# A two-layer graph network: pattern of the scatters, PSUM places of a step and the place of its additions

## The chip, the cores and the metric

The kernel runs on one core of a Trainium2 chip. The metric is the device time of one execution in microseconds, as the median of several executions.

## The reference

A graph of 6250 nodes with 128 channels and 206250 directed edges, sorted by their target `dst`, goes through two layers. The first takes the mean of the neighbours' rows, two products and a log-softmax. The second, in which the change lies, computes for each edge a weight row from 64 edge attributes (two products with a ReLU between), multiplies it with the row `h[col]` of the edge's target, and adds the result up by the edge's source.

```python
def reference(x, src, dst, edge_attr_64, ...):
    def _L1_gnn_ref(x, edge_index, edge_rbf, W1, b1, W2, b2, Wl, bl):
        weight = jnp.maximum(edge_rbf @ W1 + b1, 0.0) @ W2 + b2
        h = x @ Wl + bl
        row, col = (edge_index[0], edge_index[1])
        msg = h[col] * weight
        out = jax.ops.segment_sum(msg, row, num_segments=x.shape[0])
        return out
    edge_index = jnp.stack([src, dst])
    h = jnp.maximum(_layernorm(x, axis=-1), 0.0)
    x = x + _L0_gnn_ref(h, edge_index, L0_gnn_W_l, L0_gnn_W_r, L0_gnn_b)
    h = jnp.maximum(_layernorm(x, axis=-1), 0.0)
    x = x + _L1_gnn_ref(h, edge_index, edge_attr_64, L1_gnn_W1, ...)
    return x
```

## The kernel before

The work has three stages. The first two (layer 0, and the normalised rows `h` of layer 1 as three bf16 parts, `h1p`) are not touched. The third computes the messages of layer 1 and sums them by source.

**Steps.** The edges stand in 1664 tiles of 128 (NS = SB * P slots with the filling). Four tiles make a step, so G = 416 steps, of which 403 (GT) cover the edges' own tiles; all engines walk the same list of steps, written by `steps` (line 299): four single steps, then six parts (LOOPS, line 44), each of which but the first opens with 12 steps written out, followed by a loop of rounds of 16 steps, and 16 steps written out at the end. The order on each engine is written by hand in its own `layer1`, and semaphores (in `S`) tie the engines together. Index s or g is the step; `wait` leaves out waits on zero or less.

**A step on PE** (line 1282): `node_rows(s)` picks the rows `h[col]` with one-hot matrices into pHG; `ranks(s + 1)` counts, for the next step, how many edges of each source block come ahead of each edge, into pQ; `weights(s)` makes the weight rows of the step into pW (four times 128 channels, one PSUM bank; two places, used in turn); `hidden(s + 1)` and `attr_T(s + 2)` prepare the weights of later steps; then, in steps that carry an octet, `sums`.

**A step on ACT** (line 1457): `rows_copy` (line 1439, pHG to SBUF), `local_rows`, `stream_hot` (half of the one-hot rows of an octet, lines 1451 and 1455), `relu(s + 1)`, `attrT_copy(s + 2)`.

**A step on DVE** (line 1021): `block_hot(s + 2)`, `one_hot_T(s + 1)`, `stream_hot` (the other half of the octet's one-hot rows), `block_adds` of the octet before, `messages(s)` (line 989: pW times the copied rows, into the ring `outr` of U = 4 steps), and `row_places(s + 1)`, which ends with the slot numbers `idxr` of step s + 1 (line 983). That last instruction waits until the scatters that last used the same place of the ring, four steps back, have landed (line 982).

**POOL** (line 590) waits for the slot numbers, the source numbers (`local_rows`) and the messages of a step and scatters its four tiles into the stream `messages` in HBM, sorted by blocks of 128 sources: four indirect DMAs of 128 rows of 129 floats. The stream is zeroed beforehand; a scatter writes its rows or adds them, and `adding` says which of the four add. Four first steps and a first loop of 4 rounds of 12 steps use `fewer`, in turn one and two adding ones of four; a second loop of GL - 4 rounds of 12 steps (GL, line 33, is (GT - 1 - U) // (3 * U)) and the last 16 steps use the default, two of four.

**Octets.** When a part of the edges has been scattered, its part of the stream is read back while the next part is computed: an octet is eight tiles of it, loaded by SP (line 427) and summed by source on PE with one-hot matrices (`sums`, line 1272) into pFL, one PSUM bank with four sums of pairs of tiles; DVE adds each to its block of X (`block_adds`, line 1010, four additions, line 1016, whose block numbers are loaded into registers first). In a loop, three steps of four carry an octet. In these steps `sums` waits until the additions of the octet before have read pFL (line 1294). The last part's octets follow behind the steps, in pF.

PSUM has eight banks: 0 pTP, 1 and 2 pHID, 3 and 4 pW, 5 pHG, 6 pQ, 7 pFL.

The lines that the change and the prediction's steps touch are 261 and 264 (places), 606 to 619 (POOL's loops), 985 to 990 (`messages`), 1021 to 1034 (DVE's order), 1238 to 1247 (`weights`) and 1282 to 1295 (PE's order).

Of the kernel before, what the change touches and what calls it, by code (L numbers as in the profile page):

```python
# [5 lines left out]
def gnn_program(nc, x, src, dst, edge_attr, W_l, W_r, b_0, W1, b1, W2, b2, Wl, bl, out):  # L6
# [7 lines left out]
    P = 128  # L14
    N, C = x.shape
# [9 lines left out]
    J = 4  # L25
    GE = J * P
    U = 4
# [15 lines left out]
    FO = 8  # L43
# [43 lines left out]
    with ctx:  # L87
# [88 lines left out]
        onesb = sb("onesb", [P, P], bf16)  # L176
# [4 lines left out]
        W2s = sb("W2s", [P, C], fp32)  # L181
# [35 lines left out]
        hidT = part(big, used, 2 * GE).rearrange("p (s e) -> p s e", s=2)  # L217
        hgs = part(big, used, 2 * GE).rearrange("p (s f) -> p s f", s=2)
        outr = part(big, used, U * J * ROW).rearrange("p (u j c) -> p u j c", u=U, j=J)
# [23 lines left out]
        PS = pb("PS", [P, 8, 512], fp32)  # L243
# [14 lines left out]

        pTP = PS[:, 0, 0:2 * P].rearrange("p (q e) -> p q e", q=2)
        pHID = PS[:, 1:3, 0:2 * P]  # L260
        pW = PS[:, 3:5, :]
        pHG = PS[:, 5, :]
        pQ = PS[:, 6, 0:5 * NBK].rearrange("p (j b) -> p j b", j=5)
        pFL = PS[:, 7, :]
        pF = PS[:, 0:4, :]

        names = """raw_in w_in consts srcs_ready big_zero keys_ready keys_out offs_out off_in off_ready
# [18 lines left out]
        def wait(eng, s, v):  # L286

            if not (isinstance(v, int) and v <= 0):
                eng.wait_ge(s, v)
# [186 lines left out]
        def _(pool):  # L476
# [113 lines left out]
            def scatter(g, n, adding=(1, 3)):  # L590
                if not isinstance(g, int):
                    pool.wait_ge(S["rank_chain"], placed)
                    pool.reg_add(placed, placed, 5)
                    pool.wait_ge(S["lrow_ready"], lrows)
                    pool.reg_add(lrows, lrows, 1)
                    pool.wait_ge(S["msg_done"], filled)
                    pool.reg_add(filled, filled, 1)
                else:
                    pool.wait_ge(S["rank_chain"], 5 * g + 5)
                    pool.wait_ge(S["lrow_ready"], g + 1)  # L600
                    pool.wait_ge(S["msg_done"], g + 1)
                for j in range(J):
                    pool.indirect_dma_start(strm_d, bass.IndirectOffsetOnAxis(ap=idxr[:, n % U, j:j + 1], axis=0),  # L603
                                            outr[:, n % U, j, :], None, compute_op=ALU.add if j in adding else ALU.bypass).then_inc(S_sc[n % U], 16)
# [9 lines left out]
                    scatter(None, U + k, fewer[k % 2])  # L614
            with pool.Fori(0, GL - RINGS * LOOPS[0] // 3):
                for k in range(3 * U):
                    scatter(None, U + k)
            for g in range(U + GL * 3 * U, G):
                scatter(g, g)

# [9 lines left out]
        def _(dve):  # L630
# [339 lines left out]
            def row_places(g, n):  # L970
                k, s = n % U, n % 2
                dve.wait_ge(S["rank_done"], g + 1)
                wait(dve, S["rank_chain"], g * 5)
                nc.vector.tensor_tensor(place[:, 0, :, :], pQ[:, 0:J, :], taken.unsqueeze(1).to_broadcast([P, J, NBK]), ALU.add)\
                    .then_inc(S["rank_chain"], 1)
                dve.wait_ge(S["rank_chain"], g * 5 + 1)
                nc.vector.tensor_tensor(place[:, 1, :, :], place[:, 0, :, :], hotW[:, s, 1:, :], ALU.mult).then_inc(S["rank_chain"], 1)
                dve.wait_ge(S["rank_chain"], g * 5 + 2)
                nc.vector.tensor_reduce(place_f, place[:, 1, :, :], AX, ALU.add).then_inc(S["rank_chain"], 1)
                nc.vector.tensor_tensor(taken, taken, pQ[:, J, :], ALU.add).then_inc(S["rank_chain"], 1)  # L980
                dve.wait_ge(S["rank_chain"], g * 5 + 3)
                wait(dve, S_sc[k], (g - k) * 16)
                nc.vector.tensor_copy(idxr[:, k, :], place_f).then_inc(S["rank_chain"], 1)  # L983

            def messages(g, n):
                k = n % U
                dve.wait_ge(S["w_done"], g + 1)
                dve.wait_ge(S["hgc_done"], g + 1)
                nc.vector.tensor_tensor(outr[:, k, :, 0:C], pW[:, k % 2, :].rearrange("p (j c) -> p j c", j=J),  # L989
                                        hgs[:, k % 2, :].rearrange("p (j c) -> p j c", j=J), ALU.mult).then_inc(S["msg_done"], 1)  # L990

            one_hot_T(0, 0)
# [17 lines left out]
            def block_adds(i, sums):  # L1010
                dve.load(pair_regs, bq_i[0:1, ds(i * (FO // 2), FO // 2)])
                ats = [dve.snap(pair_regs[r], min_val=0, max_val=(NB - 1) * C) for r in range(FO // 2)]
                dve.wait_ge(S["finmm_done"], i + 1)
                for r, at in enumerate(ats):
                    wait(dve, S["fadd_done"], i * (FO // 2) + r)
                    nc.vector.tensor_tensor(Xf[:, ds(at, C)], Xf[:, ds(at, C)], sums[:, r * C:(r + 1) * C], ALU.add)\  # L1016
                        .then_inc(S["fadd_done"], 1)

            adding = [None]

            def layer1(s, n, o):
                more = not isinstance(s, int) or s + 1 < G
                if not isinstance(s, int) or s + 2 < G:
                    block_hot(s + 2, n + 2)
                if more:
                    one_hot_T(s + 1, n + 1)
                if o:
                    stream_hot(*o)
                if adding[0]:
                    block_adds(adding[0][0], pFL)  # L1030
                adding[0] = o
                messages(s, n)
                if more:
                    row_places(s + 1, n + 1)

            def next_part(p):
                dve.wait_ge(S["rank_chain"], 5 * TURN[p - 1])
# [15 lines left out]
        def _(pe):  # L1053
# [184 lines left out]
            def weights(g, n):  # L1238
                k = n % U
                pe.wait_ge(S["relu_done"], g + 1)  # L1240
                wait(pe, S["msg_done"], g - 1)
                nc.tensor.matmul(pW[:, k % 2, :].rearrange("p (j c) -> p j c", j=J), onesb[0:3, :],  # L1242
                                 bp[:, 2, :].unsqueeze(1).to_broadcast([3, J, C]), start=True, stop=False)
                for j in range(J):
                    last = nc.tensor.matmul(pW[:, k % 2, j * C:(j + 1) * C], hidT[:, k % 2, j * P:(j + 1) * P], W2s[:, :],  # L1245
                                            start=False, stop=(j == J - 1))
                last.then_inc(S["w_done"], 1)

# [33 lines left out]
            def layer1(s, n, o):  # L1282
                k = n % U
                known = isinstance(s, int)
                node_rows(s, k)
                if not known or s + 1 < G:
                    ranks(s + 1, n + 1)
                weights(s, k)
                if not known or s + 1 < G:
                    hidden(s + 1, (k + 1) % U)  # L1290
                if not known or s + 2 < G:
                    attr_T(s + 2, (k + 2) % U)
                if o:
                    wait(pe, S["fadd_done"], o[0] * (FO // 2))
                    sums(*o, pFL)

            steps(pe, layer1)

# [199 lines left out]
```

## Time and profile before

| | us |
|---|---|
| median of 3 executions | 3839.27 |
| lowest, highest | 3835.75, 3843.43 |
| the profiled execution | 3873.64 |
| its span, first to last instruction | 3871.5 |
| busy: PE, DVE, POOL, ACT | 3140.0, 2756.7, 2322.5, 2022.3 |
| POOL's scatters (line 603), 1664 | 2151.4 |

The profile is of one execution on the chip. A row of a timeline gives the start in us from the first instruction, the duration in us, the engine, the line, the operation, what it writes and reads, how many were merged, and in brackets how long the engine had been idle and what ended that. A wait is put down to the engine whose signal came last; "issue" is time in which the engine waited for nothing that the profile shows, and "remote" a signal whose sender isn't known. PE's ends are modelled. Register loads, waits and the issuing of DMAs are not counted as busy time; on POOL the scatter's own instruction is.

### The profile page before, as it was taken

Reading aid. Unit: us, or ns where it says so; the run is one execution under the profiler, and the core shown is the slowest. Engines: PE = TensorE matmul, PEld = TensorE weight load, DVE = VectorE, ACT = ScalarE, POOL = GpSimd, SP = SyncE. Lnnn points to the kernel's source line nnn. Section 1 sums busy time; section 2 is a strip of 40 time slices with the busy share of each in tenths; the row PEclk is TensorE's granted clock in tenths of the full one; section 3 lists DMA queues with packets and bytes.
Section 4 is the critical chain, followed back from the end, with each engine's and each line's share of the span. In section 5 each row is a group of like instructions: output and inputs, shape, how many; then the busy total and the mean of one; then the engine's idle time right before and its main releaser. Section 6 shows DMA issues by size and latency. Waiting matters only on the chain.

```text
span 3871.5 us, 95963 instructions
## 1 busy us (share of the span) xinstructions
PE 3140.0 (81%) x26010; PEld 2539.7 (66%) x26011; DVE 2756.7 (71%) x7612; ACT 2022.3 (52%) x4679; POOL 2322.5 (60%) x1790
## 2 busy tenths in 40 slices
PE   1799999997677888887888877888788887888867
PEld 1699999996455566665666656666566665666656
DVE  8899999997654466665666666666566665666646
ACT  2699899984422244544444444444344443444456
POOL 4310100102377778888887788888888888888830
PEclk9999999997777688998898989899898998999989
DMA  3399999201144466666676666666666666666757
GB/s 105 96 331 322 319 320 321 90 3 34 38 83 81 82 144 135 147 128 136 139 149 133 137 129 147 145 139 141 127 144 142 141 142 122 144 142 141 151 131 207
DMA packets 578296, 572.22 MB, mean 148 GB/s; under 512 B 69883, under 2 KB 562035, under 8 KB 577986
## 3 DMA queue, kind: packets, MB, share of 16 engines
q1 hardware_dynamic: 431314, 449.42, 40.9%
q0 software_dynamic: 146672, 119.07, 20.4%
q8 instruction: 147, 2.41, 0.3%
q14 instruction: 163, 1.33, 0.1%
HBM read 283.37 MB, written 284.85 MB: 147 GB/s over the span
## 4 chain that ended last, share of the span: by engine, by line
PE 46%; issue 18%; DVE 13%; POOL 7%; ACT 5%; another core or an unknown queue 5%; DMA 4%; DVEq 2%; ACTq 0%; SPq 0%; POOLq 0%
PE PS L1278 10%; PE PS L1115 10%; PE PS L1245 7%; POOL messages L603 6%; PE PS L1257 5%; PE PS L1106 4%; PE PS L1234 3%; DMA messages<-big,idxr 3%; DVE aux L767 2%; ACT big L1451 2%; DVE X L1016 2%; PE PS L1242 2%; PE PS L1226 2%; ACT hpar L1455 1%
## 5 line engine op out<-in xcount | busy, mean ns | idle before, releaser
L603 POOL DMA_INDIRECT messages<-big,idxr x1664 | 2151.4, 1293 | 570.5 <-issue 467.7
L1278 PE MATMUL PS<-big,hpar 128*128 128x128 f32 x4800 | 661.5, 295 | 227.8 <-ACT hpar L1455 120.9
L1278 PEld LDWEIGHTS PS<-big,hpar 128*128 128x128 f32 x4800 | 618.6, 208 | 278.4 <-issue 248.3
L1439 ACT ACTIVATE big<-PS 128x512 f32<-128x512 f32 x416 | 248.5, 597 | 986.3 <-PE PS L1257 635.1
L989 DVE TENSOR_TENSOR big<-PS,big 128x512 f32<-128x512 f32 x416 | 287.4, 691 | 474.9 <-PE PS L1245 222.2
L1115 PE MATMUL PS<-h_parts,counts 128*128 128x258 f32 x3626 | 565.0, 296 | 0.0
L1245 PE MATMUL PS<-W2s,big 128*128 128x128 f32 x3328 | 557.9, 318 | 0.0
L1355 ACT ACTIVATE counts<-PS 128x784 fp32r<-128x784 f32 x592 | 481.8, 825 | 119.1 <-PE PS L1106 115.0
L1245 PEld LDWEIGHTS PS<-W2s,big 128*128 128x128 f32 x3328 | 468.8, 218 | 108.5 <-issue 108.5
L1428 ACT ACTIVATE big<-PS,b1c 128x512 f32<-128x512 f32 x416 | 283.7, 682 | 455.7 <-PE PS L1234 247.7
L1016 DVE TENSOR_TENSOR X<-X,PS 128x128 f32 x1200 | 345.2, 288 | 247.8 <-PE PS L1278 84.3
L1115 PEld LDWEIGHTS PS<-h_parts,counts 128*128 128x128 f32 x3626 | 469.9, 191 | 0.2 <-ACT counts L1355 0.2
L1257 PE MATMUL PS<-hpar,big 128*128 x4992 | 418.0, 230 | 56.2 <-issue 53.8
L507 POOL DMA_INDIRECT KLg<-edge_keys,tj_i x37 | 69.8, 1886 | 625.4 <-PE PS L1086 597.8
L1257 PEld LDWEIGHTS PS<-hpar,big 128*128 128x128 bf16 x4992 | 362.6, 103 | 94.0 <-issue 65.4
L767 DVE TENSOR_TENSOR aux<-iotaLq,cols 128x1024 bf16<-128x1024 bf16 x592 | 407.9, 689 | 0.4
L1451 ACT ACTIVATE big<-iotaF,big 128x128 f32<-128x128 f32 x1200 | 380.7, 390 | 42.9 <-DMA big<-messages 41.2
L1106 PE MATMUL PS<-aux 128*128 128x98 bf16 x4736 | 316.4, 211 | 62.0 <-DVE aux L767 58.1
L1234 PE MATMUL PS<-big,W1s 64*128 64x256 f32 x1664 | 343.1, 494 | 0.0
L767 DVE TENSOR_TENSOR aux<-iotaKq,cols 128x784 bf16<-128x784 bf16 x592 | 342.2, 578 | 0.0
L1264 PE MATMUL PS<-big,onesb 128*128 128x250 bf16 x416 | 122.0, 293 | 242.3 <-DVE idxr L983 116.8
L1106 PEld LDWEIGHTS PS<-aux 128*128 128x128 bf16 x4736 | 243.1, 99 | 99.4 <-DVE aux L767 77.1
(222 smaller groups left out, 3768.4 us busy)
## 6 DMA issues: line engine op xcount, KB each, us to landing
messages<-zeros SPq DMA_DIRECT2D x843, 193.5 KB
big<-messages SPq DMA_DIRECT2D x300, 516.0 KB
aux<-slot_rows SPq DMA_DIRECT2D x416, 128.0 KB
big<-in_edge_attr_dram SPq DMA_DIRECT2D x402, 128.0 KB
messages<-big,idxr POOLq DMA_INDIRECT x1664
X<-in_x_dram SPq DMA_DIRECT2D x12, 448.0 KB, 7.2
out_dram<-X SPq DMA_DIRECT2D x6, 448.0 KB
edge_places<-big SPq DMA_DIRECT2D x1, 2496.0 KB, 13.3
```

What stands on the lines that cost most here:

```text
L603: pool.indirect_dma_start(strm_d, bass.IndirectOffsetOnAxis(ap=idxr[:, n % U, j:j + 1], axis=0), outr[:, n % U, j, :], None, compute_op=AL ...
L767: last = nc.vector.tensor_tensor(oh[:, o % NOH, :, :, :], numbers.unsqueeze(1).to_broadcast([P, Q // few, width, few]), cols[:, n % 2, w, ...
L989: nc.vector.tensor_tensor(outr[:, k, :, 0:C], pW[:, k % 2, :].rearrange("p (j c) -> p j c", j=J), hgs[:, k % 2, :].rearrange("p (j c) -> p ...
L1016: nc.vector.tensor_tensor(Xf[:, ds(at, C)], Xf[:, ds(at, C)], sums[:, r * C:(r + 1) * C], ALU.add)\
L1106: last = nc.tensor.matmul(psB[:, o % 2, s, 0:KD], ohl[:, o % NOH, s // IL, :, s % IL], ohk[:, o % NOH, s // IK, :, s % IK], start=True, st ...
L1115: last = nc.tensor.matmul(psD[:, h, :], Bc[h][:, b, :], h0p[:, b, :], start=(b == 0), stop=(b == NB - 1))
L1234: last = nc.tensor.matmul(pHID[:, h, :].rearrange("p (q e) -> p q e", q=2), W1s[h * R:(h + 1) * R, :], attrT[h * R:(h + 1) * R, k % 2, :, ...
L1245: last = nc.tensor.matmul(pW[:, k % 2, j * C:(j + 1) * C], hidT[:, k % 2, j * P:(j + 1) * P], W2s[:, :], start=False, stop=(j == J - 1))
L1257: last = nc.tensor.matmul(pHG[:, j * C:(j + 1) * C], oht[:, k % 2, j * P:(j + 1) * P], h1p[:, ds(at + a * C, C)], start=(a == 0), stop=(a ...
L1278: last = nc.tensor.matmul(to[:, r * C:(r + 1) * C], finhot[:, n % 2, r * 2 + q, :], fin[:, k, r, q * ROW:q * ROW + C], start=(q == 0), sto ...
L1355: nc.scalar.activation(Bc[h][:, :, o * Q * D:(o + 1) * Q * D].rearrange("p b (s d) -> p b s d", s=Q), psB[:, o % 2, :, 0:KD].rearrange("p ...
L1451: last = nc.scalar.activation(away[:, t, :], iotaF[:, :], ACT.Abs, bias=fin[:, k, r, q * ROW + C:(q + 1) * ROW])
```

## The change

POOL's second loop gets the pattern of its first: in turn one and two adding scatters of four. pW shrinks to one bank, so that `weights` of step g waits until `messages` of step g - 1 have read it, instead of step g - 2. The bank that comes free becomes a second place of pFL, used in turn by the octets, so that `sums` waits for the additions of the octet before last. In DVE's order `block_adds` moves from ahead of `messages` to the end of the step, behind `row_places`.

```diff
--- before.py
+++ after.py
@@ -258,10 +258,10 @@
 
         pTP = PS[:, 0, 0:2 * P].rearrange("p (q e) -> p q e", q=2)
         pHID = PS[:, 1:3, 0:2 * P]
-        pW = PS[:, 3:5, :]
+        pW = PS[:, 3, :]
         pHG = PS[:, 5, :]
         pQ = PS[:, 6, 0:5 * NBK].rearrange("p (j b) -> p j b", j=5)
-        pFL = PS[:, 7, :]
+        pFL = [PS[:, 4, :], PS[:, 7, :]]
         pF = PS[:, 0:4, :]
 
         names = """raw_in w_in consts srcs_ready big_zero keys_ready keys_out offs_out off_in off_ready
@@ -614,7 +614,7 @@
                     scatter(None, U + k, fewer[k % 2])
             with pool.Fori(0, GL - RINGS * LOOPS[0] // 3):
                 for k in range(3 * U):
-                    scatter(None, U + k)
+                    scatter(None, U + k, fewer[k % 2])
             for g in range(U + GL * 3 * U, G):
                 scatter(g, g)
 
@@ -986,7 +986,7 @@
                 k = n % U
                 dve.wait_ge(S["w_done"], g + 1)
                 dve.wait_ge(S["hgc_done"], g + 1)
-                nc.vector.tensor_tensor(outr[:, k, :, 0:C], pW[:, k % 2, :].rearrange("p (j c) -> p j c", j=J),
+                nc.vector.tensor_tensor(outr[:, k, :, 0:C], pW.rearrange("p (j c) -> p j c", j=J),
                                         hgs[:, k % 2, :].rearrange("p (j c) -> p j c", j=J), ALU.mult).then_inc(S["msg_done"], 1)
 
             one_hot_T(0, 0)
@@ -1026,12 +1026,12 @@
                     one_hot_T(s + 1, n + 1)
                 if o:
                     stream_hot(*o)
-                if adding[0]:
-                    block_adds(adding[0][0], pFL)
-                adding[0] = o
                 messages(s, n)
                 if more:
                     row_places(s + 1, n + 1)
+                if adding[0]:
+                    block_adds(adding[0][0], pFL[adding[0][1] % 2])
+                adding[0] = o
 
             def next_part(p):
                 dve.wait_ge(S["rank_chain"], 5 * TURN[p - 1])
@@ -1238,11 +1238,11 @@
             def weights(g, n):
                 k = n % U
                 pe.wait_ge(S["relu_done"], g + 1)
-                wait(pe, S["msg_done"], g - 1)
-                nc.tensor.matmul(pW[:, k % 2, :].rearrange("p (j c) -> p j c", j=J), onesb[0:3, :],
+                wait(pe, S["msg_done"], g)
+                nc.tensor.matmul(pW.rearrange("p (j c) -> p j c", j=J), onesb[0:3, :],
                                  bp[:, 2, :].unsqueeze(1).to_broadcast([3, J, C]), start=True, stop=False)
                 for j in range(J):
-                    last = nc.tensor.matmul(pW[:, k % 2, j * C:(j + 1) * C], hidT[:, k % 2, j * P:(j + 1) * P], W2s[:, :],
+                    last = nc.tensor.matmul(pW[:, j * C:(j + 1) * C], hidT[:, k % 2, j * P:(j + 1) * P], W2s[:, :],
                                             start=False, stop=(j == J - 1))
                 last.then_inc(S["w_done"], 1)
 
@@ -1291,8 +1291,8 @@
                 if not known or s + 2 < G:
                     attr_T(s + 2, (k + 2) % U)
                 if o:
-                    wait(pe, S["fadd_done"], o[0] * (FO // 2))
-                    sums(*o, pFL)
+                    wait(pe, S["fadd_done"], (o[0] - 1) * (FO // 2))
+                    sums(*o, pFL[o[1] % 2])
 
             steps(pe, layer1)
 
```

## Rows read from the trace of the kernel before

**Rows 1.** The page: span, busy time by engine, slices of POOL.

```profile
span 3871.5 us, 95963 instructions
...
PE 3140.0 (81%) x26010; PEld 2539.7 (66%) x26011; DVE 2756.7 (71%) x7612; ACT 2022.3 (52%) x4679; POOL 2322.5 (60%) x1790
...
POOL 4310100102377778888887788888888888888830
```

**Rows 2.** Windows: stretch, us; busy us (count) of PE, PEld, DVE, ACT, POOL; clock, DMA, GB/s.

```profile
1066.00:1372.00 306.00, 245.66 (x1392) 165.59 (x1392) 150.22 (x481) 79.81 (x191) 232.56 (x192) 0.72 0.44 83
1400.00:2030.00 630.00, 516.88 (x3905) 396.46 (x3903) 417.73 (x1315) 286.88 (x725) 510.56 (x393) 0.90 0.68 140
2030.00:2200.00 170.00, 143.88 (x1017) 110.82 (x1018) 109.25 (x342) 76.74 (x195) 130.82 (x103) 0.85 0.64 135
2200.00:3540.00 1340.00, 1095.07 (x8321) 838.31 (x8321) 891.48 (x2793) 605.44 (x1537) 1087.04 (x831) 0.91 0.67 139
```

**Rows 3.** POOL's timeline: start, us, instruction, idle time before; first loop of scatters.

```profile
1107.24 0.98 POOL L603 DMA_INDIRECT messages<-big,idxr  x1 [0.31 <-issue]
...
1109.79 1.60 POOL L603 DMA_INDIRECT messages<-big,idxr  x1 [0.30 <-issue]
...
1114.24 1.66 POOL L603 DMA_INDIRECT messages<-big,idxr  x1 [0.30 <-issue]
...
1117.49 1.57 POOL L603 DMA_INDIRECT messages<-big,idxr  x1 [0.30 <-issue]
1119.36 0.98 POOL L603 DMA_INDIRECT messages<-big,idxr  x1 [0.30 <-ACT big L1433]
```

**Rows 4.** POOL's timeline in the second loop of scatters.

```profile
2040.25 0.98 POOL L603 DMA_INDIRECT messages<-big,idxr  x1 [0.30 <-issue]
2041.54 1.56 POOL L603 DMA_INDIRECT messages<-big,idxr  x1 [0.30 <-issue]
...
2052.86 0.97 POOL L603 DMA_INDIRECT messages<-big,idxr  x1 [0.30 <-issue]
```

**Rows 5.** Timeline, all engines: scatters that ran beside an issue of SP.

```profile
1879.15 0.38 SPq L427 DMA_DIRECT2D big<-messages  x1
1879.26 1.23 POOL L603 DMA_INDIRECT messages<-big,idxr  x1 [0.30 <-issue]
...
2003.02 2.01 POOL L603 DMA_INDIRECT messages<-big,idxr  x1 [0.30 <-issue]
```

**Rows 6.** Waits from 1380 to 3600 us: who <- whom, us, times, longest.

```profile
POOL messages L603 <- issue: 388.3, 1273, 0.7
...
DVE idxr L983 <- DMA messages<-big,idxr: 144.7, 100, 5.5
...
DVE X L1016 <- PE PS L1278: 71.9, 86, 2.4
...
POOL messages L603 <- DVE big L989: 23.3, 51, 1.6
...
PE PS L1278 <- DVE X L1016: 15.4, 19, 1.4
```

**Rows 7.** Timeline of all engines over one step with an octet.

```profile
1882.19 0.69 DVE L989 TENSOR_TENSOR big<-PS,big 128x512 f32<-128x512 f32 x1 [0.74 <-PE PS L1245]
...
1882.56 2.02 PE L1278 MATMUL PS<-big,hpar 128*128 128x128 f32 x16 [0.81 <-ACT hpar L1455]
...
1883.98 0.17 DVE L983 CAST idxr<-big 128x4 int32<-128x4 f32 x1
...
1885.25 0.28 PE L1264 MATMUL PS<-big,onesb 128*128 128x250 bf16 x1
...
1885.96 1.55 DVE L1016 TENSOR_TENSOR X<-X,PS 128x128 f32 x4
...
1888.37 1.80 PE L1278 MATMUL PS<-big,hpar 128*128 128x128 f32 x14 [0.35 <-ACT hpar L1455]
1888.70 0.69 DVE L989 TENSOR_TENSOR big<-PS,big 128x512 f32<-128x512 f32 x1 [1.19 <-remote]
```

## The prediction

> **What bounds the kernel now.** I read the page first, for the share of each engine and for the slices, then the windows of the third stage (the 416 steps of four tiles each), then POOL's timeline, then the waits, and last one step of all engines. On the page POOL is busy for only 60% of the span and PE for 81% [rows 1], which would name PE. The slices say otherwise: POOL's digits are 7 to 9 from the twelfth slice to the next to last, and POOL counts as idle in the 0.30 us before each scatter, which no other engine ends [rows 3, 4]. Adding that: a step has four scatters, and between 1400 and 2030 us POOL issued 393 of them in 630 us, busy 510.56 us [rows 2]; 393 x 0.30 us = 118 us of issue makes 628.5 of 630 us. POOL does nothing else than scatter, back to back. 393/4 = 98.25 steps in 630 us are 6.41 us a step; from 2200 to 3540 us it is 1340/207.75 = 6.45. I use 6.43.
>
> The waits agree. POOL waited for the products (line 989) 23.3 us in 2220 us, and its own issue makes 388.3 us; in the other direction, DVE's write of the next slot numbers (line 983) stood 144.7 us, 100 times, until a scatter had landed [rows 6]. The rest of the step runs ahead of POOL and is held back by the ring of four. Spread over the (3600 - 1380)/6.43 = 345 steps of that window this is 0.42 us a step: an estimate of what the other engines have in hand. The exception is 2030 to 2200 us: 103 scatters in 170 us, 6.60 us a step, with TensorE's granted clock at 0.85 of full speed [rows 2]; there the others had fallen back and POOL waited.
>
> **The scatters.** The change gives the steps of POOL's second loop the pattern that its first loop has. GL is (403 - 1 - 4) // 12 = 33, the first loop takes 4 rounds, so 29 rounds x 12 = 348 steps move from two accumulating scatters of four to three of eight; the last 16 steps stay. Number and bytes of the scatters stay too. Both patterns stand in the trace without a disturbance. With three of eight, eight scatters take from 1107.24 to 1119.36 us, 12.12 us [rows 3]; with four of eight, from 2040.25 to 2052.86 us, 12.61 us [rows 4]. That is 6.06 against 6.305 us a step, 0.245 us less. It is less than the plain difference of one scatter: an accumulating one takes 1.56 us and a plain one 0.98 [rows 4], 0.58 us per two steps, but behind two plain ones the accumulating one took 1.60 and 1.66 us, and the one behind a single plain one 1.57 [rows 3]. So 348 x 0.245 = 85 us, and without that after-effect 174 x 0.58 = 101 us; I take 85, since the after-effect is in the rows of the same pattern.
>
> The measured 6.43 is 0.125 us above the undisturbed 6.305. Part of it are scatters that ran long while SP issued another DMA: a plain one of 1.23 us started 0.11 us after the issue of a stream load [rows 5]. The number of stream loads a step doesn't change, so I keep the whole 0.125 us; the first loop has no stream loads and can't show whether it grows. New floor of POOL: 6.06 + 0.125 = 6.185 us a step.
>
> **Whether the others follow.** 0.245 us a step is less than the 0.42 us they have in hand, so POOL stays the bound on average. But what is in hand isn't spread evenly: the stretch at 2030 to 2200 us had none, and 170/6.6 = 26 steps there gain nothing, 26 x 0.245 = 6 us. With a faster POOL such stretches start earlier and last longer. I count them twice over, 13 us, and a floor between none and the whole gain is what the range has to carry.
>
> **One PSUM place for the weights** (lines 1241 to 1246, 989). `weights` of step s now waits until the products of step s - 1 have been read. Ahead of it on PE's queue stand `node_rows` and `ranks` of s + 1, and `ranks` already waits for the slot numbers of step s, which DVE makes after the products of step s - 1, in order. In the step shown, DVE's line 983 starts at 1883.98 us, `ranks` (line 1264) runs at 1885.25, and the products ahead of line 983 had started at 1882.19 [rows 7]: the new wait is met before PE comes to it. Cost 0; were the order of PE's queue another, it would be the 0.69 us of the products a step, on PE.
>
> The Trainium skill speaks against this edit: Perfetto Trace Analysis, section Matmuls, says that independent matmul groups should rotate through different PSUM banks, so that reading one overlaps the matmuls of the next. By that rule the 0.69 us would stand on PE in each step, which is worked out in rival (a); the trace doesn't agree, as the reading is over before the next group starts, so the sum holds 0 for it.
>
> **Two places for the sums, additions last in the group** (lines 264, 1029 to 1034, 1294). `sums` now waits for the additions of the octet before last. The wait that this loosens is small: PE stood 15.4 us for line 1016 in the whole window; what `sums` waits for is mostly ACT's one-hot rows. DVE stood 71.9 us for `sums` ahead of the additions [rows 6], and the products stood behind them on DVE's queue. Moved behind `row_places`, the additions (four of 0.29 us and their gaps, 1.55 us [rows 7]) find their sums long done, and the products and slot numbers, which POOL wants, come up to 1.55 us earlier in a step with additions. Queued behind the additions are now `block_hot`, `one_hot_T` and DVE's half of `stream_hot` of the next step. DVE runs through the same instructions between two products as before, one set of additions each time, so its round gets no longer; in the step shown it had 1.19 us to spare ahead of line 989 [rows 7]. The four register loads of `block_adds` come along; they don't show in the trace. Before, they lay behind `stream_hot` without a gap; behind line 983 they may be exposed: between 0 and, with 1.19 us spare, about that much a step at no cost. While POOL is the bound, all this is worth nothing directly except in the waits of POOL for line 989: at most their 23.3 us [rows 6]. I count 0 and leave 23 us in the range.
>
> **The sum.** -85 (scatters) + 13 (stretches in which the others are late) + 0 + 0 = -72 us. The profiled execution took 3873.6 us with a span of 3871.5 [rows 1], which becomes 3802; it lies 34 us above the median of 3839.3, and nothing in the edits depends on that, so I take the same 72 us off the median: 3767.
>
> **Rivals.**
> (a) The others become the bound. In the step with an octet, the start of `sums` to the next start is 1888.37 - 1882.56 = 5.81 us [rows 7], and the granted clock is 0.90 to 0.91 of full on average and 0.85 in the late stretch [rows 2]. If sums, copies and loop starts together allow only about 6.33 us a step (the middle between the floor and the late stretch, rounded: (6.06 + 6.60)/2), the gain is 348 x 0.10 = 35 us: 3804. For it: the pace of 6.60 at 2030 us. Against: the 144.7 us in which DVE was held by the ring. A form of it is the products' 0.69 us laid on PE's queue: the step with an octet is then 6.50 us, the one without 6.50 - 2.02 = 4.48 [rows 7], three to one (3 x 6.50 + 4.48)/4 = 6.00 us: still under POOL's 6.185, with less in hand, and by the same share of late stretches it would end between the forecast and 3804. I give this form 0.02 of the 0.17. It is what the Trainium skill's rule on rotating PSUM banks (Perfetto Trace Analysis, Matmuls) would make of this kernel.
> (b) The edits do nothing for the time: the others were at 6.43 already, and the ring waits are only the even ground of a chain in step with POOL. 3839. Against: POOL's gaps, 0.30 us each time, and nothing else in them.
> (c) Slower: plain scatters leave a backlog, and the accumulating one behind two of them waits for it. With three of eight, two of three stand so, 1.0 a step; without stream loads they took 1.60 and 1.66 us, 1.63 in the mean [rows 3]. The 0.245 us is used up when they take 1.63 + 0.245 = 1.875 us. A single accumulating one beside an issue of SP took 2.01 us already [rows 5]; were that the rule for those behind two plain ones, it would be (2.01 - 1.63 - 0.245) x 348 = +47 us: 3886. Against: without the loads the rise is only 0.06 us.
> (d) More than forecast: no after-effect and POOL's waits for line 989 gone: -101 - 23 = -124: 3715.
>
> **How the numbers follow.** Forecast 0.66, (a) 0.17, (b) 0.05, (c) 0.07, (d) 0.05. Most likely 3767. The range of 8 in 10 takes in (a) and the best part of (d): 3725 to 3815. A measurement of this kernel can tell some 0.2%, 8 us, from no change. Faster by more: 0.66 + 0.17 + 0.05 = 0.88; within: 0.05; slower: 0.07.
>
> **What would show it.** In the profile after, POOL's scatters should number some 6.2 us for four in the middle stretches, with 0.30 us before nearly all; the pattern in the timeline is that of rows 3. DVE's wait for landed scatters should fall from 144.7 to some 60 us; line 1016 should wait for PE hardly at all, and line 989 should start earlier in steps with additions. No wait for line 989 should appear ahead of line 1242. If POOL's waits for line 989 rise to over 60 us, it is (a); if the accumulating scatters behind two plain ones take over 1.87 us, it is (c). The forecast is wrong if the mean scatter doesn't fall from 1.30 to about 1.24 us.

## The result: 4.4% slower

The changed kernel takes 4007.1 us (median of four executions, 4000.6 to 4012.6) against 3837.9 of the kernel before (four executions): a ratio of 1.0438, with an interval of 1.0424 to 1.0453. The prediction was 3767.

Page of the kernel after: span, busy time by engine, slices of POOL, and the group of the scatters (busy us, mean ns of one | idle us before them, what ended most of it).

```profile
span 4010.2 us, 95964 instructions
...
PE 3163.3 (79%) x26010; PEld 2577.5 (64%) x26011; DVE 2742.1 (68%) x7612; ACT 2018.2 (50%) x4679; POOL 2226.1 (56%) x1790
...
POOL 4211100103577777677766776677767667766740
...
L603 POOL DMA_INDIRECT messages<-big,idxr x1664 | 2053.6, 1234 | 807.6 <-issue 442.9
```

The same group on the page of the kernel before:

```profile
L603 POOL DMA_INDIRECT messages<-big,idxr x1664 | 2151.4, 1293 | 570.5 <-issue 467.7
```

What was forecast of POOL itself came: the mean scatter fell from 1293 to 1234 ns and their sum by 97.8 us. But POOL's idle time before them rose by 237.1 us. The difference, 139.3 us, is that of the two profiled spans, 4010.2 - 3871.5 = 138.7 us. (The profiled execution of before, 3873.6 us, lay 36 us above the median of 3837.9, that of after only 5.5 above its own, so the medians differ by more, 169 us.)

Windows of after, with the columns of [rows 2]:

```profile
1400.00:2030.00 630.00, 494.95 (x3638) 384.30 (x3637) 384.36 (x1220) 266.01 (x679) 453.63 (x369) 0.89 0.60 130
2200.00:3540.00 1340.00, 1051.41 (x7711) 813.08 (x7709) 818.96 (x2596) 562.57 (x1432) 958.07 (x776) 0.89 0.60 129
```

776/4 = 194 steps in 1340 us are 6.91 us a step, where [rows 2] gave 6.45. The granted clock of TensorE is 0.89 of full speed, against 0.90 to 0.91.

Waits of after from 1380 to 3600 us (who <- whom: us, times, longest), as [rows 6]:

```profile
ACT big L1439 <- remote: 452.2, 104, 6.5
POOL messages L603 <- issue: 338.9, 1086, 1.1
...
POOL messages L603 <- DVE big L989: 289.5, 176, 5.0
...
DVE X L1016 <- issue: 155.9, 229, 1.1
PE PS L1278 <- ACT hpar L1455: 155.2, 78, 4.8
...
PE PS L1278 <- DVE hpar L1005: 60.7, 37, 4.9
...
DVE idxr L983 <- DMA messages<-big,idxr: 3.1, 3, 1.3
```

The ring is no longer full: DVE's line 983 waits 3.1 us for landed scatters instead of 144.7. POOL waits 289.5 us for the messages of line 989 instead of 23.3. The bound has changed sides: POOL is now fed too late. The same is seen in its timeline (start, us, instruction, idle time before and what ended it), where the pattern is that of [rows 3] and the gaps are new:

```profile
2041.95 1.59 POOL L603 DMA_INDIRECT messages<-big,idxr  x1 [0.30 <-issue]
2045.13 0.97 POOL L603 DMA_INDIRECT messages<-big,idxr  x1 [1.58 <-DVE big L989]
2046.54 1.57 POOL L603 DMA_INDIRECT messages<-big,idxr  x1 [0.44 <-issue]
...
2051.89 1.58 POOL L603 DMA_INDIRECT messages<-big,idxr  x1 [1.22 <-DVE big L989]
...
2056.33 1.59 POOL L603 DMA_INDIRECT messages<-big,idxr  x1 [0.30 <-issue]
2061.00 0.98 POOL L603 DMA_INDIRECT messages<-big,idxr  x1 [3.09 <-DVE big L989]
```

The accumulating scatter behind two plain ones (2041.95, 2056.33) takes 1.59 us, against 1.60 and 1.66 in [rows 3].

### The profile page after: what moved, and what is told of

Same layout as the page of the kernel before. It is cut to its first block, busy times and chain, and to the rows that moved or that the text cites. A ratio compares the mean times of both kernels' runs of the same rounds, so it can differ in the third digit from the quotient of the medians.

```text
span 4010.2 us, 95964 instructions
## 1 busy us (share of the span) xinstructions
PE 3163.3 (79%) x26010; PEld 2577.5 (64%) x26011; DVE 2742.1 (68%) x7612; ACT 2018.2 (50%) x4679; POOL 2226.1 (56%) x1790
## 4 chain that ended last, share of the span: by engine, by line
PE 44%; issue 16%; DVE 16%; another core or an unknown queue 10%; ACT 7%; POOL 3%; DVEq 2%; DMA 1%; ACTq 0%; SPq 0%; POOLq 0%
PE PS L1278 11%; PE PS L1115 9%; PE PS L1245 6%; PE PS L1257 5%; PE PS L1106 4%; ACT big L1451 3%; DVE X L1016 3%; PE PS L1234 2%; DVE aux L767 2%; POOL messages L603 2%; PE PS L1242 2%; PE PS L1226 1%; ACT hpar L1455 1%; DVE big L974 1%
## 5 line engine op out<-in xcount | busy, mean ns | idle before, releaser
L603 POOL DMA_INDIRECT messages<-big,idxr x1664 | 2053.6, 1234 | 807.6 <-issue 442.9
L1278 PE MATMUL PS<-big,hpar 128*128 128x128 f32 x4800 | 728.7, 315 | 435.1 <-ACT hpar L1455 202.2
L1278 PEld LDWEIGHTS PS<-big,hpar 128*128 128x128 f32 x4800 | 674.2, 224 | 495.2 <-issue 396.9
L1245 PE MATMUL PS<-W2s,big 128*128 128x128 f32 x3328 | 528.9, 306 | 1.6 <-issue 1.3
L1245 PEld LDWEIGHTS PS<-W2s,big 128*128 128x128 f32 x3328 | 442.6, 207 | 107.1 <-issue 107.0
L1257 PE MATMUL PS<-hpar,big 128*128 x4992 | 433.1, 238 | 43.2 <-issue 38.2
L1257 PEld LDWEIGHTS PS<-hpar,big 128*128 128x128 bf16 x4992 | 381.2, 108 | 77.8 <-issue 50.7
L1234 PE MATMUL PS<-big,W1s 64*128 64x256 f32 x1664 | 327.0, 472 | 0.0
```

The costliest lines, as they stand in the source:

```text
L1234: last = nc.tensor.matmul(pHID[:, h, :].rearrange("p (q e) -> p q e", q=2), W1s[h * R:(h + 1) * R, :], attrT[h * R:(h + 1) * R, k % 2, :, ...
L1245: last = nc.tensor.matmul(pW[:, j * C:(j + 1) * C], hidT[:, k % 2, j * P:(j + 1) * P], W2s[:, :], start=False, stop=(j == J - 1))
L1257: last = nc.tensor.matmul(pHG[:, j * C:(j + 1) * C], oht[:, k % 2, j * P:(j + 1) * P], h1p[:, ds(at + a * C, C)], start=(a == 0), stop=(a ...
L1278: last = nc.tensor.matmul(to[:, r * C:(r + 1) * C], finhot[:, n % 2, r * 2 + q, :], fin[:, k, r, q * ROW:q * ROW + C], start=(q == 0), sto ...
```

## Experiments

"Pace" below is the time of four scatters on POOL between 1400 and 3540 us, counted as in [rows 2]; runs whose before was timed on another chip are compared by ratio. The first four runs take the change apart.

**e1, the scatters' pattern alone.**

```diff
                 for k in range(3 * U):
-                    scatter(None, U + k)
+                    scatter(None, U + k, fewer[k % 2])
```

> The kernel before with the pattern of the scatters alone (three accumulating of eight in POOL's second loop); PSUM places and the order on DVE as before. Theory H (hold): PE's signals to ACT and DVE come mostly just as an accumulating scatter ends, so with fewer of these the other engines get their signals later and POOL waits: 3950 to 4010 us. Theory O (order): the additions at the end of the step, with their register loads, make the one-hot rows and so the sums late; the pattern itself does what was forecast: 3760 to 3800 us.

Measured: 3907.0 us, ratio 1.0181 [1.0144, 1.0218]; 1302 scatters in 2140 us, a pace of 6.57. The edit that was to bring all of the gain is slower by itself. Its waits (same view and window):

```profile
POOL messages L603 <- DVE big L989: 176.9, 118, 4.0
...
DVE idxr L983 <- DMA messages<-big,idxr: 5.0, 3, 2.4
```

**e2, the rest alone**, the changed kernel with the old pattern.

```diff
-                    scatter(None, U + k, fewer[k % 2])
+                    scatter(None, U + k)
```

> The changed kernel with the pattern of the scatters put back (two accumulating of four); PSUM places and the order on DVE as changed. Theory H: no slower than before, 3815 to 3845 us. Theory O: the slowdown stays, 3950 to 4010 us. Both at work: something between, 3860 to 3940 us, and then e1 lies between too.

Measured: 3842.5 us, 1.0002 [0.9990, 1.0013]; 1334 scatters, a pace of 6.42. Waits:

```profile
DVE idxr L983 <- DMA messages<-big,idxr: 225.0, 133, 5.7
...
DVE X L1016 <- issue: 144.8, 222, 1.3
...
PE PS L1278 <- DVE hpar L1005: 106.1, 71, 5.1
...
POOL messages L603 <- DVE big L989: 17.4, 57, 0.3
```

The additions stand 144.8 us behind their register loads, and the one-hot rows of DVE make `sums` wait 106.1 us, but DVE is held by the full ring for 225.0 us, so nothing of it reaches the end. e2's profiled execution is close to its median and serves as a better base than the longer one of before: the 1334 - 1237 = 97 scatters by which the changed kernel is behind in this window are 24 steps, at 6.91 us 168 us, and the spans differ by 4010.2 - 3843.0 = 167.2. For e1 it is 32 scatters, 8 steps, 53 us of 57.8. The loss lies in the second loop.

**e3, the additions put back ahead of the products, all else as after.**

```diff
+                if adding[0]:
+                    block_adds(adding[0][0], pFL[adding[0][1] % 2])
+                adding[0] = o
                 messages(s, n)
                 if more:
                     row_places(s + 1, n + 1)
-                if adding[0]:
-                    block_adds(adding[0][0], pFL[adding[0][1] % 2])
-                adding[0] = o
```

> The changed kernel with the additions put back ahead of the products; pattern and PSUM places as changed. Theory H: still slow, 3950 to 4010 us. Theory O: as forecast for the whole change, 3760 to 3800 us, with POOL's waits for line 989 under 60 us.

Measured: 3906.3 us, 1.0177 [1.0150, 1.0204], the time of e1. So the place of the additions costs 4007 - 3906 = 101 us in company of the new pattern, and nothing in e2.

**e4, the PSUM places alone**: e3 with the old pattern, the diff of e2.

> The kernel before with the PSUM places alone (one for the weights, two for the sums); pattern and order as before. Both theories: 3825 to 3845 us, the wait on the single place being met already. If one place for the weights costs what the rule on rotating banks says, 3855 us or more.

Measured: 3840.6 us, 1.0002 [0.9990, 1.0013]. Ahead of line 1242, where the new wait stands, PE waited 0.2 us in the whole window, and not for line 989. The rule that matmul groups should rotate through PSUM banks (the Trainium skill, Perfetto Trace Analysis, section Matmuls) costs nothing to break here, since `ranks` ahead of `weights` waits for something later.

So the scatters are at fault, and the next runs ask how a POOL that has less to do makes the others slower.

**e5, before without its scatters.** POOL's scatters and the waits for their landing are taken out (SP's lines 431 and 465, POOL's 606 to 619).

```diff
-            with pool.Fori(0, GL - RINGS * LOOPS[0] // 3):
-                for k in range(3 * U):
-                    scatter(None, U + k)
...
-                wait(dve, S_sc[k], (g - k) * 16)
```

> The kernel before without its scatters and without the waits for them: POOL does nothing in the third stage, and the sums are sums of a zeroed stream. What is left is the pace of the other engines by themselves. If that pace is what the forecast took it for (6.43 - 0.42 = 6.0 us a step): 1040 + 416 x 6.0 + 150 = 3685 us, 3640 to 3700 us. If the other engines alone need what they needed in e1 (6.55 us), 3890 to 3920 us: then the pattern only uncovered them, and POOL's scatters don't slow them.

Measured: 3220.4 us, 0.8383 [0.8349, 0.8417], far below both theories. Windows of e5 for line 970 alone, the products (busy us of DVE, count; clock, DMA share, GB/s):

```profile
1400.00:2800.00 1400.00, 190.99 (x277) 0.98 0.44 124
```

277 steps in 1400 us: left to themselves, the others need 5.05 us a step, at 0.98 of the full clock. In the prediction they had 0.42 us in hand below 6.43, that is about 6.0. So about a us of their step comes from POOL's scatters being there, the lower clock of 0.90 to 0.91 [rows 2] and the scatters' transfers included. The load on the DMA engines doesn't explain the order of the runs, though: between 1400 and 3540 us their busy share is 0.67 in before, 0.60 in e1 and after, and 0.42 in e6 below, the slowest of the four. In e5's timeline (lines 1238 and 1420 are 1257 and 1439 of before), ACT reads `node_rows` as soon as PE has made them:

```profile
2601.79 0.83 PE L1238 MATMUL PS<-hpar,big 128*128 x12
...
2602.66 0.60 ACT L1420 ACTIVATE big<-PS 128x512 f32<-128x512 f32 x1 [2.02 <-PE PS L1238]
```

PE's group ends at 2602.62, ACT starts at 2602.66. In the changed kernel the same pair is far apart:

```profile
2642.75 0.67 DVE L1005 TENSOR_TENSOR hpar<-iotaN,big 128x512 f32<-128x512 f32 x1
...
2643.48 2.05 PE L1278 MATMUL PS<-big,hpar 128*128 128x128 f32 x16 [1.46 <-DVE hpar L1005]
...
2649.87 0.17 DVE L983 CAST idxr<-big 128x4 int32<-128x4 f32 x1
...
2650.74 0.71 DVE L1016 TENSOR_TENSOR X<-X,PS 128x128 f32 x2 [0.70 <-issue]
2651.39 1.59 POOL L603 DMA_INDIRECT messages<-big,idxr  x1 [0.30 <-issue]
...
2651.85 0.83 PE L1257 MATMUL PS<-hpar,big 128*128 x12
...
2653.13 1.16 PE L1245 MATMUL PS<-W2s,big 128*128 128x128 f32 x8
...
2655.84 1.58 POOL L603 DMA_INDIRECT messages<-big,idxr  x1 [0.30 <-issue]
2656.06 0.60 ACT L1439 ACTIVATE big<-PS 128x512 f32<-128x512 f32 x1 [5.36 <-remote]
...
2657.57 0.69 DVE L989 TENSOR_TENSOR big<-PS,big 128x512 f32<-128x512 f32 x1 [3.35 <-remote]
...
2659.05 0.97 POOL L603 DMA_INDIRECT messages<-big,idxr  x1 [1.63 <-DVE big L989]
```

PE's `node_rows` (line 1257) end at 2652.68, and ACT, idle for 5.36 us, starts at 2656.06. PE's `weights` (line 1245) end at 2654.29, and DVE starts the products at 2657.57, 0.14 us after POOL's accumulating scatter of 2655.84 has ended. PE's semaphore events in the trace show the same as the readers: the signal is late.

**e6, all scatters of the second loop plain**, and **e7, the accumulating ones (A) and the plain ones (P) bunched**: as many of each as before, in the order A A P P P P A A.

```diff
-                    scatter(None, U + k)
+                    scatter(None, U + k, ())                          # e6
+                    scatter(None, U + k, ((0, 1), (2, 3))[k % 2])     # e7
```

> The kernel before with only plain scatters in POOL's second loop; POOL's floor there falls to 4 x (0.97 + 0.305) = 5.1 us a step, so that the other engines are the bound. Theory H (PE's signals are let through as an accumulating scatter ends, and without one they come later): slower than e1, 3920 to 4100 us. Theory B (an accumulating scatter only blocks, and fewer of them are better; e1 is slow for another reason): faster than before, 3640 to 3720 us.

> The kernel before with the same number of accumulating scatters, two of four, but bunched over two steps as A A P P, P P A A instead of P A P A. POOL's own time per step stays about 6.3 us. Theory S (what matters is the even spacing of the accumulating scatters, one end every 3.15 us): slower, 3880 to 3960 us. Theory N (their number matters, each adds POOL time or lets the others through): as before, 3825 to 3855 us.

Measured: e6 4270.9 us, 1.1118 [1.1034, 1.1202], with POOL's own busy time lowest of all (1685.9 us of scatters) and a pace of 7.68 (1115 scatters in 2140 us); e7 4062.5 us, 1.0575 [1.0474, 1.0677], with as many scatters of each kind as before, a pace of 7.05. POOL's load is not what decides; the order of plain and accumulating ones is. e6's timeline, with PE's `node_rows` and ACT's reading of them:

```profile
2608.54 0.96 POOL L603 DMA_INDIRECT messages<-big,idxr  x1 [2.08 <-DVE big L989]
...
2609.79 1.49 PE L1257 MATMUL PS<-hpar,big 128*128 x12
...
2612.33 0.96 POOL L603 DMA_INDIRECT messages<-big,idxr  x1 [0.30 <-issue]
...
2614.25 0.60 ACT L1439 ACTIVATE big<-PS 128x512 f32<-128x512 f32 x1 [6.59 <-remote]
...
2614.95 0.69 DVE L989 TENSOR_TENSOR big<-PS,big 128x512 f32<-128x512 f32 x1 [2.53 <-ACT big L1439]
...
2616.44 0.96 POOL L603 DMA_INDIRECT messages<-big,idxr  x1 [3.15 <-DVE big L989]
```

`node_rows` end at 2611.28, POOL's last scatter of the step at 2613.29, and ACT starts at 2614.25. In the trace's semaphore events five signals of PE, of matmuls that had ended between 2611.3 and 2614.1, come between 2614.23 and 2614.48. POOL then waits for the messages until 2616.44.

From the semaphore events of four of PE's signals I counted, between 1450 and 3540 us, the share that came over 0.3 us after the modelled end of their last matmul, by what POOL did at that end (in brackets how many signals):

| the matmul ended | before | after | e1 | e6 |
|---|---|---|---|---|
| within an accumulating scatter | 0.68 (619) | 0.64 (283) | 0.63 (370) | - |
| up to 0.35 us after one | 0.09 (88) | 0.28 (85) | 0.28 (122) | - |
| within a plain scatter | 0.36 (316) | 0.54 (383) | 0.58 (430) | 0.78 (386) |
| up to 0.35 us after one | 0.59 (116) | 0.68 (151) | 0.57 (125) | 0.88 (145) |
| 0.35 to 0.7 us after any | 0 (2) | 0 (18) | 0 (25) | 0.95 (39) |
| 0.7 to 1.2 us after any | 0 (1) | 0 (47) | 0 (29) | 0.47 (78) |
| later | none | 0 (88) | 0 (41) | 0 (350) |

In e5 none is late. The column of before is of its longer execution; with the same pattern, the first four shares are 0.47, 0, 0.10 and 0.29 in e2 and 0.57, 0.01, 0.07 and 0.19 in e4, so after and e1 lose more against these. And the held ones go mostly around the end of an accumulating scatter: in before, 4.7 of all PE's signals per us came in the 0.15 us behind such an end, 0.25 to 0.62 per us during plain ones; and of the signals that were over 0.3 us late, 0.75 came between 0.2 us ahead of and 0.25 us behind such an end, a stretch of 0.14 of the time. In e2 it is 0.75 too, in e1 0.56, in after 0.46. With P A P A such an end comes every 3.15 us; with the pattern of three in eight, by the ends in [rows 3], the intervals are 4.51, 3.16 and 4.45 us; with all plain ones there is none. The mean lateness of `node_rows`' signal is 0.01 us in e5, 0.53 in e2, 0.65 in e4, 1.00 in before, 1.24 in after, 1.27 in e1, 1.57 in e7 and 2.40 in e6.

**e8, after without its scatters** (the cuts of e5), and **e11, the same with the register loads of the additions ahead of `messages`.**

```diff
+                ats = add_places(adding[0][0]) if adding[0] else None    # the four register loads; e11
                 messages(s, n)
                 if more:
                     row_places(s + 1, n + 1)
                 if adding[0]:
-                    block_adds(adding[0][0], pFL[adding[0][1] % 2])
+                    block_adds(adding[0][0], pFL[adding[0][1] % 2], ats)
```

> The changed kernel without its scatters and without the waits for them: the other engines alone with the additions last and the two places for sums. If the order costs time by itself, which e2 hid because POOL was the bound there, this is 80 to 110 us slower than e5 (what the changed kernel lost against e1). If the order costs only together with POOL's pattern, it is within 15 us of e5.

> As e8 (the changed kernel without scatters), with the register loads of the additions moved ahead of the products, the additions still last. If the exposed loads (0.68 us ahead of the additions) are what the order costs: most of the 141 us between e5 and e8 goes, 3220 to 3270 us. If it is the one-hot rows of the next step, now behind the additions, for which the sums wait: 3310 to 3365 us.

Measured: e8 3361.2 us, 141 more than e5; e11 3315.8, 45 less than e8. But e11 ran on another chip, where before took 3863.8 us instead of 3838.1, and by ratio (0.8581 against 0.8750) it is some 65 us. So a third to a half of the 141 us are the loads. Waits and window of e8 (line 997 is the additions, 1259 `sums`, 986 DVE's one-hot rows), 1400 to 2800 us:

```profile
DVE X L997 <- issue: 110.0, 161, 0.7
...
PE PS L1259 <- DVE hpar L986: 79.8, 52, 4.4
```

```profile
1400.00:2800.00 1400.00, 174.85 (x255) 0.97 0.41 115
```

and the same two in e11 (lines 1263 and 1000):

```profile
PE PS L1263 <- DVE hpar L986: 59.9, 52, 6.4
...
DVE X L1000 <- issue: 2.8, 9, 0.5
```

255 steps in 1400 us are 5.49 us a step, 0.44 more than e5; PE's 79.8 us for the one-hot rows were 10.5 in e5. The additions behind `row_places` stand ahead of the one-hot rows of the next octet, and `sums` waits for these. The other 76 to 96 us I put down to that; no run moves the one-hot rows alone. In after's timeline above the two show as 0.70 us of "issue" ahead of line 1016 and 1.46 us ahead of line 1278.

**e9, plain scatters with a pause.** After the second and the fourth scatter of a step POOL clears a tile and waits for that.

```diff
+                    if j in pauses:
+                        nc.gpsimd.memset(zeros[:, :], 0.0).then_inc(S["paused"], 1)
+                        pool.wait_ge(S["paused"], paused)
+                        pool.reg_add(paused, paused, 1)
...
-                    scatter(None, U + k)
+                    scatter(None, U + k, (), (1, 3))
```

> As e6, only plain scatters in POOL's second loop, but after the second and the fourth of a step POOL clears a small tile and waits for that, some 0.6 us: POOL's rhythm is about that of P A P A, without an accumulating DMA. Theory T (any pause of POOL after a run of scatters lets PE's signals through): near the kernel before, 3820 to 3950 us. Theory A (it takes an accumulating DMA): no better than e6, 4250 us or more.

Measured: ratio 1.0778 [1.0729, 1.0827], 3.4 points better than e6 though POOL does more. The pauses came out longer than meant, 1.23 us from the end of a scatter to the next (2602.01 to 2603.24):

```profile
2601.06 0.95 POOL L605 DMA_INDIRECT messages<-big,idxr  x1 [0.30 <-issue]
2602.01 0.44 POOL L608 MEMSET zeros<- 128x387 f32 x1
2603.24 0.96 POOL L605 DMA_INDIRECT messages<-big,idxr  x1 [0.80 <-issue]
```

and with them POOL is the bound again, by its own waiting:

```profile
POOL messages L605 <- issue: 539.9, 991, 1.3
DVE idxr L989 <- DMA messages<-big,idxr: 514.7, 261, 5.4
```

DVE waits for the ring for 514.7 us, POOL hardly for the products any more, and `node_rows`' signal is late by 0.66 us in the mean. A matmul that ended over 0.7 us after a scatter was never late (0 of 208).

**e10, the accumulating ones moved by one place.**

```diff
-                    scatter(None, U + k)
+                    scatter(None, U + k, (0, 2))
```

> The kernel before with the first and third scatter of a step accumulating instead of the second and fourth: the same number and the same even spacing, another place in the step. If even spacing is what counts: 3825 to 3855 us. If the place in the step counts (signals that come due just after the last scatter): 3870 us or more.

Measured: ratio 1.0024 [1.0012, 1.0037], a pace of 6.43. With equal intervals the place within the step hardly counts.

**e12, e13 and e14, shorter pauses among plain scatters**: POOL clears the same tile as in e9 (e12) or a third of it (e13 and e14), and waits only for the clearing of the time before. From the end of a scatter to the next start it came to 0.60 us behind the second of a step in e12, 0.38 us there in e13, and 0.38 us between any two of a step in e14, shorter than the expectations have it; behind the fourth POOL mostly waited some 3 us for the messages, as in e6.

```diff
+                    if j in pauses:
+                        pool.wait_ge(S["paused"], paused)
+                        pool.reg_add(paused, paused, 1)
+                        nc.gpsimd.memset(zeros[:, 0:387], 0.0).then_inc(S["paused"], 1)    # 0:128 in e13 and e14
```

> Only plain scatters in POOL's second loop; after the second and the fourth of a step POOL clears a tile (0.43 us) without waiting for it. From the end of a plain scatter to the next one it is 0.43 + 0.305 = 0.74 us there, POOL's floor is 2 x (2 x 0.96 + 2 x 0.305 + 0.43) = 5.92 us a step. In e9, with 1.24 to 1.46 us between, PE's signals came through (0.66 us late on average for line 1257's, against 2.40 in e6). If 0.74 us is enough: POOL-bound again, 348 x (5.92 + 0.13 - 6.43) = -132 us, 3700 to 3760 us. If it isn't: slow like e6, 4000 us or more.

> As e12 with a smaller tile (0.21 us): 0.52 us from the end of a plain scatter to the next, floor 5.48 us a step. If 0.52 us is enough, 3600 to 3700 us, with the other engines near the bound; if not, 4000 us or more. With e12 and e9 it shows how long POOL must pause before PE's signals come through.

> As e13 with the pause of 0.21 us after each scatter: floor 4 x (0.96 + 0.21 + 0.305) = 5.90 us a step. If the signals wait for a pause of a certain length, it is as slow as e13; if pauses add up (each lets a few signals through), it is faster than e13 by 100 us or more, down to 3700 to 3760 us.

Measured: ratios 1.112 [1.109, 1.115], 1.120 [1.117, 1.123] and 1.119 [1.115, 1.122], no better than e6's 1.112, and `node_rows`' signal is late by 2.48, 2.54 and 2.52 us in the mean. Pauses of 0.38 to 0.60 us within a step don't help. A version that beats the kernel before was not found.

## Why the prediction was wrong

- **What bounds the kernel now**: right for before. POOL issues back to back there, and e2 and e10 keep its pace (6.42 and 6.43). (POOL's slices are misread in a detail on which nothing hangs: they are 7 and 8, and the next to last is a 3 [rows 1].)
- **The scatters themselves**: right. -85 us of busy time were forecast (-101 without the after-effect), and -97.8 came. The price of an accumulating scatter behind two plain ones held too, so rival (c) was right in its sign alone; its mechanism, a backlog that makes that scatter take over 1.87 us, isn't what happened.
- **Whether the others follow**: this step failed. The 0.42 us that they have in hand were worked out rightly from the ring waits [rows 6], but taken for a quantity of their own, which stays when POOL changes. As a size it was loose too: in e10, with POOL's pace as in before, the ring waits in the same window are 221.7 us, in e4 324.8. The runs show that the others' pace depends on POOL's order of plain and accumulating scatters: 5.05 us a step with none (e5), less than 6.43 under P A P A, 6.57 under three in eight (e1), 7.05 under e7's order, 7.68 with plain ones alone. The pattern that saves POOL 0.245 us a step leaves fewer and uneven moments at which PE's held signals mostly pass. Rival (a), the others as the bound, was right in kind, and its sign of recognition was met (over 60 us of waits for line 989: 289.5). Its price was not: its 6.33 us a step was taken from the middle between two rows, neither of which says what the others need under the new pattern.
- **A row that was passed over**: the first loop of before had the new pattern, and I read the scatters' durations from 12 us of it. It ran with POOL as the bound there [rows 3], but without octets: 1392 matmuls in 306 us, 4.5 per us, where 3905 in 630 us are 6.2 [rows 2]. So it shows POOL's floor and not whether the others, with their octets, keep up.
- **One PSUM place for the weights**: 0 forecast, 0 measured (e4).
- **Two places for the sums**: no gain looked for and none found (e4).
- **Additions last in the group**: 0 forecast, 101 us measured beside the new pattern (after against e3). That the additions would find their sums done came true: line 1016 waited 1.3 us for PE in after, where it was 71.9 [rows 6]. The argument that DVE's round "gets no longer" failed twice: the four register loads, hidden before, take 0.68 to 0.70 us each time behind line 983 (e11 gets 45 to 65 of e8's 141 us back by moving them), and the one-hot rows of the next octet now stand behind the additions, so `sums` waits. The prediction named both (loads "about that much a step at no cost", and what is queued behind the additions), but hid both under 1.19 us to spare ahead of line 989 at 1888.70 us [rows 7]. Two more lines of before show that this was no time in hand but a wait for a late signal:

```profile
1885.86 1.16 PE L1245 MATMUL PS<-W2s,big 128*128 128x128 f32 x8
...
1887.10 1.56 POOL L603 DMA_INDIRECT messages<-big,idxr  x1 [0.30 <-issue]
```

  PE's `weights` had ended at 1887.02, DVE's additions at 1887.51; the products started at 1888.70, 0.04 us after the accumulating scatter had ended, and the trace has the signal of `weights` 1.66 us after their end. While POOL is the bound such waits cover the loads (e2, 1.0002); with the pattern they don't.
- **The sum**: 68 us for the pattern (e1, 3907.0 - 3839.4) and 101 us for the order make 169 us, the measured loss, where -72 was forecast.
- **The rest**: the granted clock is 0.89 where it was 0.90 to 0.91, and 0.83 in e6. How much of the 6.91 or of the 7.68 us that is, the runs don't separate. Nor is e1's 68 us free of it: e1 has 0.90, and so has the profiled execution of before, but those of before against which e1 was timed have 0.91 to 0.92. At 0.90 before took 3873.6 us (the profiled one) and 3863.8 (the median beside e9 and e10), and e1 is still 33 to 43 us slower than these. So the pattern costs time at the same clock, and up to half of the 68 us may go with the lower one.

## What to carry to other kernels

Time in hand that is read from a wait holds for the pace and the pattern under which it was read: before an engine is given less to do, ask whether the others run at that pace in any row, here with octets and with that order of scatters. An edit that costs nothing under a bound (e2) has a price of its own; measure it with the bound taken away (e8) before it is counted at nothing. And when the idle time of an engine ends late after its sender's last instruction, compare the signal's time with that end: the loss may lie between the two.

## What the runs showed of the hardware

POOL's indirect scatters delay what PE signals to ACT and DVE. Without them every such signal came 0.01 to 0.02 us after the modelled end (e5); with them `node_rows`' signal came 0.5 (e2) to 2.5 us (e13) late in the mean, and held signals come together, as the five in e6. Around the end of an accumulating scatter most of them go: 0.75 of those over 0.3 us late in before and in e2, 0.46 in after. Behind plain ones the delay outlasts the instruction: after four in a row matmuls that ended up to 1.2 us later were still late (0.47 of those from 0.7 to 1.2 us), after two in a row ones up to 0.7 us later (e9, 0.14 of those from 0.35 to 0.7 us). The Trainium skill (SBUF — State Buffer, section SBUF: two separate sides) says that on the engines' side only the port pair shared by two of them makes anyone wait, and that PE and ACT never do; whether it is a port or not, PE's results came late here by the numbers of e5 and e6, so that rule doesn't make PE's signals safe from POOL's scatters.

Left open: by what way the scatters hold the signals. Since PE's ends are modelled, the trace doesn't tell a held semaphore from matmuls whose last results are written late; that later groups of PE start meanwhile, as at 2653.13 above, speaks for the signal. Nor was it found why 0.60 us of pause didn't help where 1.23 us did.
